# Attention stage of a transformer block on one core: the four output chunks of a quad of units spread over four iterations

## The chip, the cores and the metric

The kernel runs on one core of a Trainium2 chip. The metric is the time of one execution on the device, in microseconds (us), lower is better.

## The reference

`x` has shape (4, 512, 128). It is normalised per token; the result goes into an attention branch and into a mixture-of-experts branch, and both are added to `x`:

```python
xn = _layernorm(x, axis=-1)
x = x + attention(xn) + experts(xn)
# attention, 16 heads of 8, keys and values through a latent of 32
scores = einsum('bhqd,bhkd->bhqk', qh, kh) * scale
scores = clip(nan_to_num(scores), -1e4, 1e4) * exp(-1e-4 * |i - j|)
attn = softmax(scores, axis=-1)
out = einsum('bhqk,bhkd->bhqd', attn, vh)      # then @ Wo
# experts: top 2 of 8, exact gelu, hidden size 512, then layer norm
```

## The kernel before

All data stays in fp32; products of scores are made of bf16 parts. A first part (to about 129 us) normalises, projects, routes tokens to experts and runs the experts' matmuls. The second part, which the change touches, is the attention; it takes the branch `fast == 1` on every engine. POOL gathers the experts' results meanwhile, and VectorE, beside its share of attention, normalises the sum per batch.

**Units.** There are 4 x 16 = 64 pairs of batch and head. A *group* is 4 heads (16 groups). Each group is done in two halves, and each half has two tiles of 128 keys (`HALVES = ((0, 3), (1, 2))`). One head's half is a *unit*: 128 units, 8 a group. Four units of one half are a *quad*: 32 quads. Units 8g to 8g+3 and 8g+4 to 8g+7 are the two quads of group g. In the traces unit n is found by counting: the loads of L626 come two a unit, from unit 0 at 128.64 us.

**One loop, four engines.** Each engine runs a loop over n, written out at build time; n is called an iteration, or unit n.
- TensorE, `scores(n)` (L626): two matmuls 128x512 into banks 2(n mod 3) and the next, so three units have scores at a time. Before them it waits for `fast_probs`, that is, for the exponential of unit n-3.
- VectorE (L1043): two multiplications correct the decay in these banks in place.
- ScalarE (L811): one exponential 128x1024 writes `probs_fast`, two buffers of one quad each; it signals `fast_probs`. The first exponential of a quad waits for `fast_used`, given when the quad two before (same buffer) is done with.
- TensorE, `outputs(quad, chunk)` (L645): a quad's probabilities times values. There are four chunks: two key tiles by two halves of the queries, each with four matmuls of 9 x 256, one for each head, side by side in the output bank, and each in two passes. Chunk 0 waits for the quad's four exponentials, and in a group's first quad for `fast_heads` as well. Chunk 3 signals `fast_used`.
- ScalarE, `heads(group)` (L785): copies the output bank to `out_heads` ahead of the exponential of unit 8g+12, once both of the group's quads are used; it signals `fast_heads`.
- TensorE, `turn(group)` (L659), at iteration 8g+17: four transposes of the copied heads, after which VectorE divides by the sums (L1031, L1033).

Three batches' attention is turned and projected inside the loop, too: transposes L603 at iterations 101, 109 and 125, their copy by ScalarE (L789) ahead of the exponentials of units 100, 108 and 124, matmuls L610 two iterations after L603, and an addition by VectorE (L1014), for which the next turn waits (`out_ready`). VectorE takes statistics (L986, L992, L994) after units 58, 66, 92 and 98, and roots and scalings (L1000 to L1007) from units 84, 88, 106 and 109. After unit 127 the loop goes on for 20 iterations to finish the last chunks and turns.

Waits are on semaphores, and each engine works strictly through its own list, so what stands behind a waiting instruction waits with it. The order around the change is set by the loop at the end of TensorE's branch (L661 to L678): in each iteration come the scores of unit n, then the chunks that the tuple `((0,), (1, 2), (3,), ())` names, taken at `at`, the place of n in its quad counted from n = 6, then a turn where one is due, then the transposes and the projection of a batch.

Of the kernel before, what the change touches and what calls it, by code (L numbers as in the profile page):

```python
# [65 lines left out]
def build(nc, x_tiles, chain, w_up, w_router, rest, weights, decay, fold, mend, out):  # L66
    with ExitStack() as ctx:
# [169 lines left out]
        def batch_at(n, units, step=0):  # L237
            return units.index(n - step) if n - step in units else None
# [233 lines left out]
        def _(pe):  # L472
# [128 lines left out]
            def turn_attention(b):  # L601
                for t in range(QT):
                    last = nc.tensor.transpose(ps[:, TURN_BANK, t * P:(t + 1) * P],  # L603
                                               attn[:, b * QT + t, :, :].rearrange("p h d -> p (h d)"), ident)
                last.then_inc(attnT_psum, 1)

            def project_attention(b):
                pe.wait_ge(attnT_ready, b + 1)
                for t in range(QT):
                    last = nc.tensor.matmul(ps[:, TURN_BANK, t * D:(t + 1) * D], attnT[:, b * QT + t, :], wo_sb,  # L610
                                            start=True, stop=True)
                last.then_inc(wo_psum, 1)
# [3 lines left out]
            with pe.If(fast == 1):  # L616
                def scores(n):
                    group, half, g = n // (2 * GROUP), n // GROUP % 2, n % GROUP
                    b, h = divmod(group * GROUP + g, HEADS)
                    if n % (UNITS // B) == 0:  # L620
                        pe.wait_ge(rows_in[b % 2], (b // 2 + 1) * len(PRODUCTS) * 2 * 16)
                    if n >= SCORE_SLOTS:
                        pe.wait_ge(fast_probs, n - SCORE_SLOTS + 1)
                    for k in range(2):
                        keys = HALVES[half][k] * P
                        nc.tensor.matmul(ps[:, 2 * (n % SCORE_SLOTS) + k, :], k_rows[:, b % 2, h, keys:keys + P],  # L626
                                         q_rows[:, b % 2, h, :], start=True, stop=True).then_inc(fast_scores, 1)

                def outputs(quad, chunk):
                    k, side = divmod(chunk, 2)  # L630
                    queries = slice(side * S // 2, (side + 1) * S // 2)
                    group, half = divmod(quad, 2)
                    tile = HALVES[half][k]
                    first_tile, last_tile = (half, k) == (0, 0), (half, k) == (1, 1)
                    if chunk == 0:
                        pe.wait_ge(fast_probs, (quad + 1) * GROUP)
                    if first_tile and side == 0:
                        if group:
                            pe.wait_ge(fast_heads, group)
                        else:  # L640
                            pe.wait_ge(v_ones, 1)
                            pe.wait_ge(out_clear, 1)
                    for g in range(GROUP):
                        b, h = divmod(group * GROUP + g, HEADS)
                        last = nc.tensor.matmul(ps[32 * g:32 * g + VW, OUT_BANK, queries], v_sb[:, b * QT + tile, h, :],  # L645
                                                probs_fast[:, quad % 2, g, k * S + queries.start:k * S + queries.stop],
                                                start=first_tile and side == 0,
                                                stop=last_tile and side == 1, skip_group_check=True)
                    if chunk == 3:
                        last.then_inc(fast_used, 1)  # L650

                def turn(group):
                    pe.wait_ge(fast_heads, group + 1)
                    if group:
                        pe.wait_ge(fast_done, group)
                    if group - 1 in PROJECT_GROUPS:
                        pe.wait_ge(out_ready, PROJECT_GROUPS.index(group - 1) + 1)
                    for t in range(QT):
                        last = nc.tensor.transpose(ps[:, TURN_BANK, t * P:(t + 1) * P], out_heads[:, t * P:(t + 1) * P], ident)  # L659
                    last.then_inc(fast_outT, 1)  # L660

                for n in range(UNITS + 5 * GROUP):
                    if n < UNITS:
                        scores(n)
                    quad, at = divmod(n - GROUP - 2, GROUP)
                    if 0 <= quad < QUADS:
                        for chunk in ((0,), (1, 2), (3,), ())[at]:
                            outputs(quad, chunk)
                    group, at = divmod(n - TURN_AFTER, 2 * GROUP)
                    if 0 <= group < GROUPS and at == 0:  # L670
                        turn(group)
                    if (b := batch_at(n, PROJECT_AT)) is not None:
                        pe.wait_ge(fast_done, GROUPS if b == B - 1 else PROJECT_GROUPS[b] + 1)
                        turn_attention(b)
                    if (b := batch_at(n, MULTIPLY_AT)) is not None:
                        project_attention(b)
# [471 lines left out]
```

## Time and profile before

| what | value |
|---|---|
| median of 3 runs | 300.53 us (299.96 to 301.22) |
| the profiled execution's own time | 301.67 us |
| its span | 299.9 us |
| busy: TensorE matmul, weight loads | 250.9 us, 140.1 us |
| busy: VectorE, ScalarE, POOL | 227.9, 203.0, 167.9 us |
| mean granted clock of TensorE | 0.945 |
| exponentials (L811), 128 | 124.8 us, 1029 ns each |
| corrections (L1043), 256 | 112.9 us, 495 ns each |
| chunks (L645), 1024 records, scores (L626), 232 records | 74.5 us, 71.5 us |

PE is TensorE's matmul, PEld its weight load, DVE VectorE, ACT ScalarE. Times in a timeline count from the span's start; an entry such as [0.43 <-ACT shared L811] says how long the engine sat idle before the row, and what ended it. Neighbouring instructions of one kind are merged into one row with their count. Matmuls are pipelined, so the length of one holds its latency, and the step from one start to the next says what it occupies. Some matmul records are missing from the trace (232 of 256 for L626); the weight loads are complete.

### The profile page before, as it was taken

The page shows a single profiled execution, that of the slowest core. Times are in us where ns is not written, and L with a number is a line of the kernel's source. Part 1 is how long each engine was busy: PE and PEld are TensorE (multiplying, and loading weights), DVE is VectorE, ACT ScalarE, POOL GpSimd, SP SyncE. Part 2 cuts the span into 40 slices and gives each one's busy share as a digit, 9 for nine tenths or more (in the row PEclk, how much of TensorE's full clock was granted, in tenths as well). Part 3 has the DMA queues.
Part 4 walks back from the last instruction along what each step waited for, and adds up shares of the span by engine and source line. Part 5 has one row for each costly group of instructions (what it writes and reads, how often), then busy time and mean ns, then how long its engine had stood idle before and what let it go on. Part 6 is the DMA issues. An engine that isn't in the chain of part 4 may idle for free.

```text
span 299.9 us, 6073 instructions
## 1 busy us (share of the span) xinstructions
PE 250.9 (84%) x2161; PEld 140.1 (47%) x2185; DVE 227.9 (76%) x585; ACT 203.0 (68%) x348; POOL 167.9 (56%) x158
## 2 busy tenths in 40 slices
PE   0394457989999999969999999989999598969883
PEld 0282033979999999922222233322233023332342
DVE  3718987587777777677888888889889987998831
ACT  1556506446666665668999999988997588769840
POOL 9296707447464557968899999995305711050000
PEclk9998957899999999998999999999999789999996
DMA  6992501242222323125111531115000000000001
GB/s 212 469 388 70 164 21 44 72 159 74 79 70 70 71 71 68 35 88 185 47 35 28 169 96 31 35 52 175 11 2 2 1 0 2 35 7 31 2 35 42
DMA packets 14065, 24.37 MB, mean 81 GB/s; under 512 B 2240, under 2 KB 11104, under 8 KB 13648
## 3 DMA queue, kind: packets, MB, share of 16 engines
q1 hardware_dynamic: 11424, 19.03, 17.8%
q0 software_dynamic: 2272, 4.66, 6.4%
q8 instruction: 19, 0.31, 0.4%
q10 hardware_dynamic: 336, 0.25, 0.3%
q14 instruction: 14, 0.11, 0.1%
HBM read 12.99 MB, written 4.65 MB: 59 GB/s over the span
## 4 chain that ended last, share of the span: by engine, by line
PE 57%; DVE 23%; ACT 11%; issue 5%; DMA 2%; another core or an unknown queue 1%; ACTq 0%; DVEq 0%
PE ps L645 13%; PE ps L626 12%; PE ps L572 11%; PE ps L583 11%; ACT shared L811 9%; DVE ps L1043 8%; PE ps L659 2%; DMA wvl<-w_router 2%; DVE panels L1007 2%; PE ps L493 2%; DVE shared L908 2%; PE ps L561 1%; PE ps L610 1%; PE ps L485 1%; DVE panels L1014 1%
## 5 line engine op out<-in xcount | busy, mean ns | idle before, releaser
L811 ACT ACTIVATE shared<-ps 128x1024 f32<-128x1024 f32 x128 | 124.8, 1029 | 21.3 <-DVE ps L1043 18.6
L1043 DVE TENSOR_TENSOR ps<-ps,mend_sb 128x128 f32<-128x128 f32 (+3 forms) x256 | 112.9, 495 | 19.8 <-PE ps L626 15.3
L626 PE MATMUL ps<-stacked 128*128 128x512 bf16 x232 | 71.5, 392 | 15.1 <-ACT shared L811 12.3
L645 PE MATMUL ps<-shared,v_sb 128*9 128x256 f32 x1024 | 74.5, 388 | 0.0
L774 ACT ACTIVATE shared<-ps,shared 128x128 f32<-128x128 f32 x156 | 44.6, 369 | 32.4 <-PE ps L572 32.4
L307 POOL DMA_INDIRECT shared<-xn_scr,source_i x39 | 42.0, 1076 | 39.1 <-PE ps L561 28.3
L927 DVE COPY shared<-panels 128x1156 f32 x39 | 36.3, 930 | 14.6 <-issue 14.6
L626 PEld LDWEIGHTS ps<-stacked 128*128 128x128 bf16 x256 | 17.1, 98 | 58.8 <-ACT shared L811 36.2
L572 PE MATMUL ps<-shared 128*128 128x128 f32 x312 | 42.3, 279 | 1.3 <-DVE shared L964 1.2
L583 PE MATMUL ps<-shared 128*128 128x128 f32 x312 | 42.2, 279 | 0.3 <-ACT shared L774 0.3
L645 PEld LDWEIGHTS ps<-shared,v_sb 128*9 128x9 f32 x1024 | 18.8, 89 | 48.1 <-issue 36.3
L572 PEld LDWEIGHTS ps<-shared 128*128 128x128 f32 x312 | 38.8, 195 | 2.0 <-DVE shared L964 1.6
L583 PEld LDWEIGHTS ps<-shared 128*128 128x128 f32 x312 | 38.8, 196 | 0.5 <-ACT shared L774 0.5
L316 POOL DMA_INDIRECT panels<-y_scr,y_row x32 | 31.2, 974 | 7.9 <-issue 5.2
L346 POOL TENSOR_TENSOR panels<-panels,rest_sb 128x512 f32<-128x512 f32 x4 | 5.1, 1271 | 31.9 <-DVE panels L1007 31.9
L972 DVE TENSOR_TENSOR y_rows<-ps,shared 128x128 f32<-128x128 f32 x39 | 11.3, 291 | 8.0 <-PE ps L583 7.5
L785 ACT COPY out_heads<-ps 128x512 f32<-128x512 f32 x16 | 9.3, 584 | 6.4 <-PE ps L645 6.4
L659 PE MATMUL ps<-chain_sb,out_heads 128*128 128x128 f32 x64 | 9.7, 275 | 3.1 <-DVE panels L1014 2.3
L561 PE MATMUL ps<-chain_sb,shared 128*128 128x128 f32 x39 | 11.2, 286 | 1.1 <-DMA shared<-xn_scr,source_i 1.1
L749 ACT ACTIVATE qT_sb<-ps 128x512 f32<-128x512 f32 x4 | 2.5, 614 | 14.2 <-PE ps L512 14.2
L964 DVE COPY shared<-ps 128x128 f32<-128x128 f32 x39 | 11.0, 282 | 0.4 <-PE ps L561 0.3
L659 PEld LDWEIGHTS ps<-chain_sb,out_heads 128*128 128x128 f32 x64 | 7.7, 141 | 7.3 <-issue 3.7
(146 smaller groups left out, 245.7 us busy)
## 6 DMA issues: line engine op xcount, KB each, us to landing
stacked<-parts SPq DMA_DIRECT2D x48, 128.0 KB
panels<-weights SPq DMA_DIRECT2D x1, 4624.0 KB, 18.2
y_scr<-y_rows SPq DMA_DIRECT2D x19, 128.0 KB
x_sb<-x_tiles SPq DMA_DIRECT2D x4, 256.0 KB, 4.8
xn_scr<-x_sb SPq DMA_DIRECT2D x1, 1024.0 KB, 7.2
xnT<-x_tiles SPq DMA_DIRECT2D x1, 1024.0 KB
out<-panels SPq DMA_DIRECT2D x4, 256.0 KB, 2.3
shared<-xn_scr,source_i POOLq DMA_INDIRECT x39
```

The costliest lines, as they stand in the source:

```text
L307: nc.gpsimd.indirect_dma_start(x_rows[:, i % X_SLOTS, :], None, xn_scr, bass.IndirectOffsetOnAxis(ap=source_i[:, i:i + 1], axis=0)).then_i ...
L316: nc.gpsimd.indirect_dma_start(gathered[:, c, t, :], None, y_scr, bass.IndirectOffsetOnAxis(ap=y_row[:, at:at + 1], axis=0)).then_inc(y_ba ...
L561: nc.tensor.transpose(ps[:, 4 + i % 2, 0:P], x_rows[:, i % X_SLOTS, :], ident).then_inc(xT_psum, 1)
L572: last = nc.tensor.matmul(ps[:, s, c * P:(c + 1) * P], panel[:, i % 4, c * P:(c + 1) * P], x_cols[:, s, :], start=True, stop=True)
L583: last = nc.tensor.matmul(ps[:, Y_BANKS[i % 2], 0:D], hidden[:, i % 2, c, :], panel[:, i % 4, F + c * D:F + (c + 1) * D], start=(c == 0), ...
L626: nc.tensor.matmul(ps[:, 2 * (n % SCORE_SLOTS) + k, :], k_rows[:, b % 2, h, keys:keys + P], q_rows[:, b % 2, h, :], start=True, stop=True) ...
L645: last = nc.tensor.matmul(ps[32 * g:32 * g + VW, OUT_BANK, queries], v_sb[:, b * QT + tile, h, :], probs_fast[:, quad % 2, g, k * S + quer ...
L659: last = nc.tensor.transpose(ps[:, TURN_BANK, t * P:(t + 1) * P], out_heads[:, t * P:(t + 1) * P], ident)
L774: last = nc.scalar.activation(hidden[:, i % 2, c, :], ps[:, i % 2, c * P:(c + 1) * P], ACT.Gelu, bias=panel[:, i % 4, 2 * F + D + c:2 * F ...
L811: nc.scalar.activation(probs_fast[:, quad % 2, g, :].rearrange("p (k q) -> p k q", k=2), ps[:, 2 * (n % SCORE_SLOTS):2 * (n % SCORE_SLOTS) ...
L927: nc.vector.tensor_copy(panel[:, i % 4:i % 4 + 1, :], panels[:, bass.ds(e, 1), :]).then_inc(panel_ready, 1)
L1043: last = nc.vector.tensor_tensor(scores, scores, mend_sb[:, S - reach:], ALU.mult)
```

## The change

The four chunks of a quad run at four iterations, one each: chunk 2 moves from the second to the third, chunk 3 from the third to the fourth, which had none.

```diff
                     quad, at = divmod(n - GROUP - 2, GROUP)
                     if 0 <= quad < QUADS:
-                        for chunk in ((0,), (1, 2), (3,), ())[at]:
-                            outputs(quad, chunk)
+                        outputs(quad, at)
                     group, at = divmod(n - TURN_AFTER, 2 * GROUP)
```

TensorE's list at iterations 12 to 14, before; L626 are scores, L645 chunks (x4 is one chunk, x8 two):

```order
L626 MATMUL ps<-stacked 128x512 [waits fast_probs]
L626 MATMUL ps<-stacked 128x512
L645 MATMUL ps<-shared,v_sb 9x256 x4
L626 MATMUL ps<-stacked 128x512 [waits fast_probs]
L626 MATMUL ps<-stacked 128x512
L626 MATMUL ps<-stacked 128x512 [waits fast_probs]
L626 MATMUL ps<-stacked 128x512
L645 MATMUL ps<-shared,v_sb 9x256 [waits fast_heads,fast_probs]
L645 MATMUL ps<-shared,v_sb 9x256 x3
```

And with the change:

```order
L626 MATMUL ps<-stacked 128x512 [waits fast_probs]
L626 MATMUL ps<-stacked 128x512
L645 MATMUL ps<-shared,v_sb 9x256 x4
L626 MATMUL ps<-stacked 128x512 [waits fast_probs]
L626 MATMUL ps<-stacked 128x512
L645 MATMUL ps<-shared,v_sb 9x256 x4
L626 MATMUL ps<-stacked 128x512 [waits fast_probs]
L626 MATMUL ps<-stacked 128x512
L645 MATMUL ps<-shared,v_sb 9x256 [waits fast_heads,fast_probs]
L645 MATMUL ps<-shared,v_sb 9x256 x3
```

In iteration 12 chunk 2 stands where chunk 3 stood, and chunk 3 now comes after the scores of unit 13, ahead of those of unit 14.

TensorE's list at iterations 16 to 18, where a turn (L659) stands, before:

```order
L626 MATMUL ps<-stacked 128x512 [waits fast_probs]
L626 MATMUL ps<-stacked 128x512
L645 MATMUL ps<-shared,v_sb 9x256 x4
L626 MATMUL ps<-stacked 128x512 [waits fast_probs]
L626 MATMUL ps<-stacked 128x512
L659 MATMUL ps<-chain_sb,out_heads 128x128 [waits fast_heads]
L659 MATMUL ps<-chain_sb,out_heads 128x128 x3
L626 MATMUL ps<-stacked 128x512 [waits fast_probs]
L626 MATMUL ps<-stacked 128x512
```

And with the change:

```order
L626 MATMUL ps<-stacked 128x512 [waits fast_probs]
L626 MATMUL ps<-stacked 128x512
L645 MATMUL ps<-shared,v_sb 9x256 x4
L626 MATMUL ps<-stacked 128x512 [waits fast_probs]
L626 MATMUL ps<-stacked 128x512
L645 MATMUL ps<-shared,v_sb 9x256 x4
L659 MATMUL ps<-chain_sb,out_heads 128x128 [waits fast_heads]
L659 MATMUL ps<-chain_sb,out_heads 128x128 x3
L626 MATMUL ps<-stacked 128x512 [waits fast_probs]
L626 MATMUL ps<-stacked 128x512
```

The turn, which followed the scores of unit 17 directly, now follows chunk 3, and there are as many chunks and turns as before. The lists of ScalarE, VectorE, POOL and SP hold the same instructions in the same order in both kernels.

## Rows read from the trace of the kernel before

**Rows 1.** The page: busy time of each engine, and the chain by engine.

```profile
PE 250.9 (84%) x2161; PEld 140.1 (47%) x2185; DVE 227.9 (76%) x585; ACT 203.0 (68%) x348; POOL 167.9 (56%) x158
...
PE 57%; DVE 23%; ACT 11%; issue 5%; DMA 2%; another core or an unknown queue 1%; ACTq 0%; DVEq 0%
```

**Rows 2.** Stretches that begin and end at a group's first scores, L626 alone.

```profile
core 0: us, PE busy (x) PEld busy (x), PEclk, DMA share, GB/s
146.93:191.31 44.38, 21.71 (x73) 5.37 (x80) 1.00 0.23 66
191.31:210.12 18.81, 8.71 (x29) 1.98 (x32) 1.00 0.32 100
210.12:227.86 17.74, 8.64 (x29) 2.15 (x32) 1.00 0.01 3
227.86:243.27 15.41, 5.51 (x14) 0.96 (x16) 0.78 0.01 2
243.27:253.97 10.70, 4.60 (x15) 1.07 (x16) 1.00 0.01 2
```

**Rows 3.** Timeline of TensorE's weight loads, units 36 to 43 (start, length, merged).

```profile
169.23 0.11 PEld L626 LDWEIGHTS ps<-stacked 128*128 128x128 bf16 x2 [0.43 <-ACT shared L811]
169.77 0.12 PEld L645 LDWEIGHTS ps<-shared,v_sb 128*9 128x9 f32 x8 [0.42 <-issue]
170.32 0.55 PEld L626 LDWEIGHTS ps<-stacked 128*128 128x128 bf16 x4 [0.43 <-ACT shared L811]
...
172.03 0.11 PEld L626 LDWEIGHTS ps<-stacked 128*128 128x128 bf16 x2 [0.61 <-ACT shared L811]
172.56 0.55 PEld L645 LDWEIGHTS ps<-shared,v_sb 128*9 128x9 f32 x16 [0.42 <-issue]
173.54 0.11 PEld L626 LDWEIGHTS ps<-stacked 128*128 128x128 bf16 x2 [0.43 <-issue]
174.08 0.12 PEld L645 LDWEIGHTS ps<-shared,v_sb 128*9 128x9 f32 x8 [0.42 <-issue]
174.63 0.11 PEld L626 LDWEIGHTS ps<-stacked 128*128 128x128 bf16 x2 [0.43 <-issue]
174.86 0.57 PEld L659 LDWEIGHTS ps<-chain_sb,out_heads 128*128 128x128 f32 x4
...
176.59 0.11 PEld L626 LDWEIGHTS ps<-stacked 128*128 128x128 bf16 x2 [0.43 <-issue]
```

**Rows 4.** Timeline of ScalarE, units 36 to 43.

```profile
170.46 0.59 ACT L785 COPY out_heads<-ps 128x512 f32<-128x512 f32 x1 [0.34 <-PE ps L645]
170.94 3.78 ACT L811 ACTIVATE shared<-ps 128x1024 f32<-128x1024 f32 x4
174.93 4.07 ACT L811 ACTIVATE shared<-ps 128x1024 f32<-128x1024 f32 x4 [0.20 <-DVE ps L1043]
```

**Rows 5.** Timelines of TensorE and of VectorE, units 88 to 96.

```profile
235.25 0.60 PE L626 MATMUL ps<-stacked 128*128 128x512 bf16 x2 [2.38 <-ACT shared L811]
...
229.79 1.22 DVE L1000 TENSOR_TENSOR newton<-rstd 128x4 f32<-128x4 f32 x1
...
243.70 0.91 DVE L1043 TENSOR_TENSOR ps<-ps,mend_sb 128x128 f32<-128x128 f32 x2 [0.76 <-PE ps L626]
```

**Rows 6.** Timelines of weight loads and of ScalarE, units 100 to 103.

```profile
247.83 0.11 PEld L626 LDWEIGHTS ps<-stacked 128*128 128x128 bf16 x2 [0.43 <-ACT shared L811]
...
251.57 0.11 PEld L626 LDWEIGHTS ps<-stacked 128*128 128x128 bf16 x2 [1.12 <-ACT shared L811]
...
250.00 0.59 ACT L789 COPY kT_sb<-ps 128x512 f32<-128x512 f32 x1 [0.19 <-PE ps L603]
250.49 3.78 ACT L811 ACTIVATE shared<-ps 128x1024 f32<-128x1024 f32 x4
```

**Rows 7.** Timeline of weight loads at unit 127 and after.

```profile
286.23 0.97 PEld L610 LDWEIGHTS ps<-rest_sb,kT_sb 128*128 128x128 f32 x8 [0.43 <-issue]
...
288.24 0.42 PEld L659 LDWEIGHTS ps<-chain_sb,out_heads 128*128 128x128 f32 x4 [0.80 <-issue]
```

## The prediction

> **What bounds the kernel now.** I read the page first: TensorE is busy for 84% of the span, VectorE 76, ScalarE 68, and the chain that ended last lies 57% on TensorE with 11% on ScalarE [rows 1]. No engine is full, so the bound has to be read inside the stage that the change touches. The stretches by group of 8 units come next [rows 2]: five groups take 44.38 us, 8.88 each, two more take 17.74, 8.87 each; the two groups with statistics on VectorE take 9.41 each, and the later ones 15.41 and 10.70. A group of 8.87 us is the regular case, and I take it apart.
>
> TensorE's weight loads tell where each piece of its program begins [rows 3]. The load at 169.23 belongs to the scores of unit 36, the first unit of a second quad. From the scores and one chunk to the next scores is 1.09 us (173.54 to 174.63), from the scores and two chunks 1.51 (172.03 to 173.54). Units 37 and 38, one without a chunk and one with, take 1.71 (170.32 to 172.03), of which 0.18 is a wait: that load sat idle 0.61 us until ScalarE had finished, where loads behind a chunk otherwise sit idle 0.43. So scores alone cost 1.71 - 0.18 - 1.09 = 0.44. A turn costs 176.59 - 174.63 - 0.44 - 1.09 = 0.43. TensorE's own demand in a group is then 2 x (1.09 + 1.51 + 1.09 + 0.44) + 0.43 = 8.69, and with the wait of 0.18 it is 8.87, the measured period. **The regular group is bound by TensorE's order, with one short wait for ScalarE in it.**
>
> Where does that wait come from? Unit 36's scores are loaded at 169.23, its chunk 3 (of the quad before) at 169.77 [rows 3]. Chunk 3's signal lets ScalarE copy the heads at 170.46, the exponential of unit 36 follows at 170.94 [rows 4] and lasts 1.03; 0.05 after its end, at 172.03, TensorE may load the scores of unit 39, which take the same score banks. The path is 0.54 + 0.69 + 0.48 + 1.03 + 0.05 = 2.79 long, TensorE's work beside it 1.09 + 0.44 + 1.09 = 2.62: 0.17 of wait, as seen.
>
> **The change, part by part.** It removes and adds no arithmetic: 128 chunks as before. It moves chunk 2 behind the next unit's scores, and chunk 3 likewise. VectorE, ScalarE, POOL and SP keep their order and their instructions, and no DMA is moved.
>
> (a) Switches. Two chunks together cost 1.51 - 1.09 = 0.42 for the second, and one set apart costs 1.09 - 0.44 = 0.65. So splitting the pair costs 0.23 a quad. TensorE's demand in a group becomes 8 x 1.09 + 0.43 = 9.15, 0.46 more. I have no row for a turn that directly follows a chunk; between nothing extra and one more switch (0.1, half of the 0.23) I take nothing, since loads from one matmul shape to another behind a chunk sit idle 0.43 whichever follows [rows 7]: the turn pays the switch that the scores would have paid.
>
> The Trainium skill (TensorE: Matmul & The Clock Gate, "The mechanism" in Part 3) says that TensorE pulls a weight load ahead of matmuls in flight when it goes to rows that don't conflict or to the background buffer. By that rule the added switches would be free and the group's demand would stay near 8.69; the trace speaks against it here, since every first load of a chunk stands idle 0.42 us behind scores [rows 3].
>
> (b) The release. Chunk 3 now stands behind the scores of unit 37, not of unit 36, so the path above grows by one unit: 1.09 + 2.79 = 3.88. Queued behind the waiting heads copy on ScalarE is the exponential of unit 36, and for that wait, three units on, the scores of unit 39. TensorE's work beside the path is 3 x 1.09 = 3.27. The wait becomes 0.61. The first quad of a group has no copy: its exponential waits for chunk 3 directly, 1.09 + 0.54 + 0.69 + 1.03 + 0.05 = 3.40, against 3.27 + 0.43 (the turn falls there) of work. No wait there, with 0.3 to spare.
>
> A regular group: 9.15 + 0.61 = 9.76, **0.89 more than 8.87**. VectorE's work of about 7.5 us a group fits inside, and ScalarE catches up, its exponentials following each other by 0.92 (four take 3.78 [rows 4]).
>
> (c) The irregular groups. In the first 16 units the wait arises once and one switch is added: +0.6. With statistics, ScalarE now waits for chunk 3 longer than for VectorE, so 9.76 takes the place of 9.41: +0.35 each, +0.7 for two. From unit 84 VectorE is the bound (square roots at 1.22 us for a tiny operation, while POOL works [rows 5]); the change has by then added 0.2 in that group, and the 0.7 that it would add is swallowed: TensorE stood idle 2.38 us there [rows 5]. Out of that stretch TensorE comes at a lower clock (mean 0.78 of full [rows 2], so partly at 1.2 GHz after that idling) and is late for VectorE by 0.76 [rows 5]; chunk 3 and its switch cost +0.3 (0 to 0.8). At unit 100 ScalarE has a second copy, of the turned attention, that TensorE's chunk 3 now precedes: scores at 247.83, exponential at 250.49, 2.66 later [rows 6]; one chunk more ahead of those transposes is +0.65, less what TensorE saves around it: +0.5. Units 104 to 115 wait for VectorE and for the projection's bank: +0.2. Units 112 to 115 end with one chunk fewer done, -0.4. One more regular group +0.9, unit 124 as unit 100, +0.7. In the tail the chunk left over runs while TensorE would sit idle (0.80 us before the turn at 288.24 [rows 7]): -0.4.
>
> Sum: 0.6 + 5 x 0.89 + 0.7 + (0.9 + 0.2) + 0.3 + 0.5 + 0.2 - 0.4 + 0.9 + 0.7 - 0.4 = 8.65, the (0.9 + 0.2) being the groups from 210.12 to 227.86. I take 8.5. The profiled execution took 301.67 us (span 299.9), which gives 310.2 for it. It is 1.14 above the median of the runs, 300.53; against the median the forecast is **309.0 us**. A difference under 0.5% (1.5 us) can't be told from none here.
>
> **The rivals.**
> - *Only the switches cost.* If ScalarE's late release is hidden, a regular group takes 9.15, +0.28, and groups bound elsewhere nothing: 5 x 0.28 + 2 x 0.28 + about 0.6 for the rest = 2.6, so 303.1. For it: ScalarE is busy for only 68% [rows 1]. Against: the 2.79 path is met to 0.01 by the present wait. 0.07.
> - *Only the release costs.* With added switches free, the group takes 9.76 - 0.46 = 9.30, +0.43, half of the forecast: 304.8. The rule quoted above on weight loads would make this the outcome. Against: the 0.42 idle loads. 0.07.
> - *The clock falls more.* TensorE will wait 0.6 us in each group and longer from unit 84. The stretch that idles now shows 0.78 [rows 2]; at half speed a unit's 1.09 becomes 2.18. Three more such units cost 3.3: 312.3. Against: a wait of 0.6 is far below the 2.38 us seen before the fall. 0.06.
> - *Faster.* Place: the first scores of each quad. They come 0.42 earlier, since the pair no longer stands before them, and ScalarE's stall there (four exponentials begun at 170.94, the next four at 174.93, so 3.99 where 4 x 0.92 = 3.68 would do [rows 4]) goes: 0.3 a quad, 0.6 a group, 8 regular groups, 4.8 us: 295.7. It decides only if TensorE's demand falls below 8.87 with the split, that is if a split pair costs under 0.09 instead of 0.23, and if the buffer is free earlier than chunk 3 says. 0.02. The two effects cancelling within 0.5%: 0.03.
>
> **How the numbers follow.** The forecast's own case has 0.75; its terms could each be off by a few tenths: with the turn's extra switch (10 x 0.1) and the upper end after the slow clock (0.5) it reaches 310.5 to 311; with 0.75 instead of 0.89 a group and nothing at 100 and 124 it is about 306.5. The range takes in the case of free switches and leaves out the others, 0.18: **304.7 to 311.3**. Slower by over 0.5% 0.95, within 0.5% 0.03, faster 0.02.
>
> **What would show it.** In the changed profile a regular group takes 9.7 to 9.8 us; the weight loads of scores and chunks alternate at 1.09; the scores of unit 39 sit idle about 1.04 (0.43 + 0.61) for ScalarE; the heads copy begins 2.3 after the scores of unit 36 instead of 1.2. ScalarE's wait for L645 before the copy grows from 0.34 [rows 4] to about 1 us, and one of about 0.7 appears before the first exponential of the quad without a copy. A copy that is late without a late load of unit 39 would be the first rival; loads of chunks not idle behind scores the second; a granted clock under 1.00 between 146 and 200 us the third. A period at or under 8.87 would refute the sum.

## The result, and the profile after

The changed kernel takes 306.88 us (306.8 to 307.08, 4 runs) where the kernel before, run beside it, takes 300.88 (299.96 to 301.37): a ratio of 1.0204, with a 95% interval of 1.0177 to 1.0232. It is 6.0 us slower; 309.0 was forecast, 304.7 to 311.3 the range.

| | before | after |
|---|---|---|
| profiled execution, its span | 301.67, 299.9 us | 306.8, 305.0 us |
| mean granted clock of TensorE | 0.945 | 0.972 |
| regular group of 8 units | 8.87 us | 9.79 us |
| ScalarE idle ahead of the heads copies (L785, now L784) | 6.4 us | 14.9 us |

The changed kernel's page: busy time by engine, and the chain that ended last by engine. One line of code has gone, so ScalarE's and VectorE's lines are one lower (L810 for L811, L784 for L785); the scores' L626, the chunks' L645 and the turn's L659 are the same.

```profile
PE 257.6 (84%) x2185; PEld 134.2 (44%) x2185; DVE 228.8 (75%) x585; ACT 200.6 (66%) x348; POOL 166.8 (55%) x158
...
PE 66%; DVE 18%; ACT 8%; issue 4%; DMA 3%; POOL 0%; ACTq 0%; DVEq 0%
```

The chain has moved further onto TensorE (66% for 57%) and off ScalarE and VectorE [rows 1]. By group, in stretches cut as in [rows 2], scores alone:

```profile
core 0: us, PE busy (x) PEld busy (x), PEclk, DMA share, GB/s
145.82:194.79 48.97, 24.15 (x80) 4.94 (x80) 1.00 0.21 62
194.79:214.37 19.58, 9.66 (x32) 1.98 (x32) 1.00 0.29 89
214.37:233.96 19.59, 9.66 (x32) 1.98 (x32) 1.00 0.01 3
233.96:248.08 14.12, 5.45 (x16) 1.02 (x16) 0.88 0.01 2
248.08:259.32 11.24, 4.82 (x16) 1.07 (x16) 1.00 0.01 1
```

Five regular groups take 48.97 us, 9.79 each. The groups with statistics (194.79 to 214.37) take the same 9.79, and the next two as well; only then does VectorE set the time again. The timeline of TensorE's weight loads at units 36 to 44, which answers to [rows 3]:

```profile
170.24 0.11 PEld L626 LDWEIGHTS ps<-stacked 128*128 128x128 bf16 x2 [0.43 <-issue]
170.78 0.12 PEld L645 LDWEIGHTS ps<-shared,v_sb 128*9 128x9 f32 x8 [0.42 <-issue]
171.33 0.11 PEld L626 LDWEIGHTS ps<-stacked 128*128 128x128 bf16 x2 [0.43 <-issue]
...
172.41 0.11 PEld L626 LDWEIGHTS ps<-stacked 128*128 128x128 bf16 x2 [0.43 <-issue]
173.25 0.15 PEld L645 LDWEIGHTS ps<-shared,v_sb 128*9 128x9 f32 x8 [0.73 <-issue]
174.12 0.11 PEld L626 LDWEIGHTS ps<-stacked 128*128 128x128 bf16 x2 [0.71 <-ACT shared L810]
...
176.83 0.12 PEld L645 LDWEIGHTS ps<-shared,v_sb 128*9 128x9 f32 x8 [0.42 <-issue]
177.38 0.42 PEld L659 LDWEIGHTS ps<-chain_sb,out_heads 128*128 128x128 f32 x4 [0.43 <-issue]
...
180.03 0.11 PEld L626 LDWEIGHTS ps<-stacked 128*128 128x128 bf16 x2 [0.43 <-issue]
```

Scores and single chunks alternate at 1.09. The load at 172.41 is unit 38's, and behind it chunk 0 waits for the heads copy (idle 0.73 where 0.42 is the switch), then the load of unit 39's scores for ScalarE (0.71): 3.88 lies between 170.24 and 174.12, where it was 2.80. From 170.24 to the same place of the next group, 180.03, is 9.79. The turn at 177.38 stands behind a chunk and is idle 0.43, as the scores would be. ScalarE in the same stretch, as in [rows 4]:

```profile
172.55 0.58 ACT L784 COPY out_heads<-ps 128x512 f32<-128x512 f32 x1 [1.00 <-PE ps L645]
173.04 3.78 ACT L810 ACTIVATE shared<-ps 128x1024 f32<-128x1024 f32 x4
177.58 3.77 ACT L810 ACTIVATE shared<-ps 128x1024 f32<-128x1024 f32 x4 [0.76 <-PE ps L645]
```

The heads copy begins 2.31 after unit 36's scores and is idle 1.00 before it, for 0.34; the first exponential of the other quad is idle 0.76 for chunk 3, where it had waited 0.20 for VectorE.

### The profile page after: what moved, and what is told of

It is laid out like the page before. It is cut to its first block, busy times and chain, and to the rows that moved or that the text cites. A ratio compares the mean times of both kernels' runs of the same rounds, so it can differ in the third digit from the quotient of the medians.

```text
span 305.0 us, 6097 instructions
## 1 busy us (share of the span) xinstructions
PE 257.6 (84%) x2185; PEld 134.2 (44%) x2185; DVE 228.8 (75%) x585; ACT 200.6 (66%) x348; POOL 166.8 (55%) x158
## 4 chain that ended last, share of the span: by engine, by line
PE 66%; DVE 18%; ACT 8%; issue 4%; DMA 3%; POOL 0%; ACTq 0%; DVEq 0%
PE ps L645 18%; PE ps L626 17%; PE ps L572 11%; PE ps L583 11%; ACT shared L810 6%; DVE ps L1042 4%; PE ps L659 3%; DMA wvl<-w_router 2%; PE ps L493 2%; PE ps L561 2%; DVE shared L907 1%; DVE panels L1006 1%; PE ps L610 1%; PE ps L485 1%; ACT out_heads L784 1%
## 5 line engine op out<-in xcount | busy, mean ns | idle before, releaser
L810 ACT ACTIVATE shared<-ps 128x1024 f32<-128x1024 f32 x128 | 122.3, 1033 | 23.1 <-PE ps L645 11.5
L1042 DVE TENSOR_TENSOR ps<-ps,mend_sb 128x128 f32<-128x128 f32 (+3 forms) x256 | 114.1, 494 | 26.9 <-PE ps L626 26.2
L626 PE MATMUL ps<-stacked 128*128 128x512 bf16 x256 | 77.5, 386 | 11.3 <-ACT shared L810 10.9
L645 PE MATMUL ps<-shared,v_sb 128*9 128x256 f32 x1024 | 79.4, 385 | 2.9 <-ACT out_heads L784 2.9
L307 POOL DMA_INDIRECT shared<-xn_scr,source_i x39 | 41.1, 1053 | 38.4 <-PE ps L561 27.4
L626 PEld LDWEIGHTS ps<-stacked 128*128 128x128 bf16 x256 | 16.3, 97 | 59.9 <-ACT shared L810 40.4
L645 PEld LDWEIGHTS ps<-shared,v_sb 128*9 128x9 f32 x1024 | 15.9, 88 | 56.8 <-issue 55.9
L784 ACT COPY out_heads<-ps 128x512 f32<-128x512 f32 x16 | 9.4, 585 | 14.9 <-PE ps L645 14.9
L341 POOL TENSOR_TENSOR rstd<-newton,top 128x4 f32<-128x4 f32 x4 | 4.1, 1023 | 16.8 <-DVE newton L993 16.8
L659 PE MATMUL ps<-chain_sb,out_heads 128*128 128x128 f32 x64 | 10.5, 286 | 1.8 <-DVE panels L1013 1.1
```

Of the source, the lines that this page charges most:

```text
L307: nc.gpsimd.indirect_dma_start(x_rows[:, i % X_SLOTS, :], None, xn_scr, bass.IndirectOffsetOnAxis(ap=source_i[:, i:i + 1], axis=0)).then_i ...
L810: nc.scalar.activation(probs_fast[:, quad % 2, g, :].rearrange("p (k q) -> p k q", k=2), ps[:, 2 * (n % SCORE_SLOTS):2 * (n % SCORE_SLOTS) ...
L1042: last = nc.vector.tensor_tensor(scores, scores, mend_sb[:, S - reach:], ALU.mult)
```

## The experiments

Each experiment is an edit of the kernel before (of the changed one where it says so), and each is read first by one regular group, units 72 to 79. The first fence of an experiment is that stretch (its start and end, its length, then the scores' records in it and the granted clock), as in [rows 2]; a second one is its timeline of weight loads, as in [rows 3]; rows of other engines say so by their names. The kernel before ran beside them and had a median of 301.50, 301.57 and 300.71 us in the three series.

**A switch more, the release where it was.** Chunk 1 runs between the two score matmuls of its unit.

```diff
                     for k in range(2):
                         keys = HALVES[half][k] * P
+                        if k and n >= 7 and n % GROUP == 3:
+                            outputs(n // GROUP - 1, 1)
...
-                        for chunk in ((0,), (1, 2), (3,), ())[at]:
+                        for chunk in ((0,), (2,) if n < UNITS else (1, 2), (3,), ())[at]:
```

> The pair of chunks 1 and 2 is split inside its own iteration: chunk 1 goes between the two score matmuls of that unit, chunk 2 behind them, so there is one more switch pair a quad but chunk 3, and with it the release of the buffer and of the heads copy, stays where it was in the kernel before. Theory (switches 0.46 a group and release 0.44 a group, added up): a regular group takes 8.87 + 0.46 = 9.33 us, the wait before the scores of unit 39 stays at 0.17, time about 303.5 to 304.5. Rival 'only the late release costs': the group stays at 8.87 and the time at 300.9. Rival 'only the switches cost': the group takes as long as in the changed kernel, 9.79, and the time is near 306.9.

```profile
213.30:222.62 9.32, 5.00 (x16) 1.22 (x16) 1.00 0.03 9
```

```profile
168.04 0.10 PEld L628 LDWEIGHTS ps<-stacked 128*128 128x128 bf16 x1 [0.43 <-issue]
168.36 0.12 PEld L647 LDWEIGHTS ps<-shared,v_sb 128*9 128x9 f32 x8 [0.23 <-issue]
168.91 0.10 PEld L628 LDWEIGHTS ps<-stacked 128*128 128x128 bf16 x1 [0.43 <-issue]
169.23 0.12 PEld L647 LDWEIGHTS ps<-shared,v_sb 128*9 128x9 f32 x8 [0.23 <-issue]
169.78 0.11 PEld L628 LDWEIGHTS ps<-stacked 128*128 128x128 bf16 x2 [0.43 <-issue]
```

(L628 is the scores, L647 a chunk here.) The group takes 9.32, 0.45 more than before, as the theory has it; from 168.04 to 169.78 are 1.74 for a unit whose pair is split, where the pair took 1.51: 0.23 a switch pair, with nothing else moved. The time was expected at 303.5 to 304.5 and came out at 307.71 (ratio 1.0232, 1.0189 to 1.0275). The regular groups are right and the rest is not: the two groups with statistics take 20.35 us for 18.81, the first 16 units 18.68 with the clock at 1.00. Two places show in the trace. Unit 7 is the first whose scores are split; the second half reaches VectorE late, its correction begins at 135.62 and ends at 137.88, where in the second profile of the kernel before it is 135.62 and 136.52, and its exponential starts 1.28 later than there. In the first group with statistics a small VectorE instruction (newton<-mv, L994 before, L996 here) takes 1.15 for 0.17, which is no part of the split; the next experiment shows what holds it up.

**The release later, no switch more.**

```diff
-                        for chunk in ((0,), (1, 2), (3,), ())[at]:
+                        for chunk in ((0,), (1, 2), (), (3,))[at]:
```

> Chunk 3 alone runs one iteration later, the pair stays together: no switch is added. Theory: path of 3.88 us against 0.44 + 1.09 + 1.09 = 2.62 of TensorE's work beside it, so a wait of 1.26; a regular group takes 8.69 + 1.26 = 9.95, 1.08 more than before and more than in the changed kernel (9.79); time about 308 to 309. Rival 'only the switches cost': 8.87 a group and 300.9. Rival 'the release costs what it costs in the changed kernel, 0.44': 9.31 a group, about 304.

```profile
215.36:224.71 9.35, 4.49 (x16) 1.15 (x16) 1.00 0.01 2
```

```profile
169.98 0.55 PEld L626 LDWEIGHTS ps<-stacked 128*128 128x128 bf16 x4 [0.43 <-issue]
...
172.34 0.15 PEld L645 LDWEIGHTS ps<-shared,v_sb 128*9 128x9 f32 x8 [0.73 <-issue]
173.21 0.11 PEld L626 LDWEIGHTS ps<-stacked 128*128 128x128 bf16 x2 [0.72 <-issue]
```

9.35 a group, 0.48 more than before. My 9.95 was wrong by an error of counting: the unit whose chunk 3 left has scores alone, 0.44 and not 1.09, so the path is 0.44 + 2.79 = 3.23. The trace has 3.23, from 169.98 to 173.21. Against 2.62 of work that is a wait of 0.61, the same as in the changed kernel, and the rival that said so was right in its figure. The time is 307.66 (1.0184, 1.0128 to 1.024). The two groups with statistics take 21.95 us of it for 18.81, more than the release's 0.48 each. 1.48 of that is one instruction:

```profile
199.27 1.65 DVE L994 TENSOR_SCALAR newton<-mv 128x4 f32<-128x4 f32 x1
```

```profile
199.71 1.17 POOL L287 TENSOR_TENSOR folded<-folded,parts 128x512 f32<-128x512 f32 x1
```

VectorE's L994 took 0.17 in the first profile of the kernel before. Here it takes 1.65 and ends at 200.92, 0.04 after POOL's L287 does. It is the same in the split above (1.15) and in the second profile of the kernel before (0.67): both ended 0.04 after a POOL TENSOR_TENSOR. The second of the two groups has a granted clock of 0.90 besides.

These two decide the main question. One switch pair a quad costs 0.45 a group, the later release 0.48, and both together, in the changed kernel, 0.92. The times alone would not have decided it: 307.71, 307.66 and the changed kernel's 306.88 to 308.98 lie within 2 us of each other, since the stretches outside the regular groups differ as well.

**The pair is chunks 2 and 3.**

```diff
-                        for chunk in ((0,), (1, 2), (3,), ())[at]:
+                        for chunk in ((0,), (1,), (2, 3), ())[at]:
```

> Chunks 1; 2 and 3; none: the pair is chunks 2 and 3, as many switches as before, chunk 3 in its old iteration but behind chunk 2. Theory: the release is 0.42 later (path 3.21), but TensorE's work beside the path grows by the same chunk (1.51 + 0.44 + 1.09 = 3.04), so the wait stays 0.17, a regular group 8.87, the time within 0.5% of 300.9. Rival 'what costs is that a chunk stands behind the next unit's scores (chunk 2 does here too)': part of the change's 6 us, 302 to 304.

```profile
211.00:219.87 8.87, 4.66 (x16) 1.08 (x16) 1.00 0.03 11
```

8.87, the period of before, and a time of 299.99 (0.9953, 0.9918 to 0.9988). Three of its groups between units 32 and 55 take 9.1 to 9.6 in the profile, which I can't place. Moving chunk 2 behind the next scores costs nothing in itself, and a release that is 0.42 later costs nothing when TensorE has 0.42 more to do beside it.

**Two pairs.**

```diff
-                        for chunk in ((0,), (1, 2), (3,), ())[at]:
+                        for chunk in ((0, 1), (), (2, 3), ())[at]:
```

> Chunks 0 and 1 together in the first iteration, 2 and 3 together in the third: one switch pair a quad fewer than before, two fewer than in the changed kernel. Theory: demand 8.69 - 0.46 = 8.23 a group; the release path is 3.21 against 1.51 + 0.44 + 1.51 = 3.46, no wait; a unit's own round (scores, correction, exponential, 2.46) against 0.44 + 1.51 + 0.44 = 2.39 adds up to 0.14: a regular group takes 8.3 to 8.4, the time 296 to 297.5. Rival 'switches are free': 8.87 or more a group, since chunks in pairs only make the scores come less evenly, 300.9 to 303.

```profile
210.25:218.93 8.68, 4.55 (x16) 1.07 (x16) 1.00 0.07 23
```

```profile
218.94 0.11 PEld L626 LDWEIGHTS ps<-stacked 128*128 128x128 bf16 x2 [0.66 <-ACT shared L811]
```

```profile
215.54 1.02 ACT L811 ACTIVATE shared<-ps 128x1024 f32<-128x1024 f32 x1 [0.45 <-DVE ps L1043]
216.46 0.58 ACT L785 COPY out_heads<-ps 128x512 f32<-128x512 f32 x1
```

8.68, less than the 8.87 of before, so switches are not free; but not 8.3 to 8.4. The load at 218.94 is the scores of unit 80, idle 0.66 for ScalarE. The third fence is ScalarE: the exponential of unit 75 and, right behind it, the heads copy. The other regular groups of this profile are less even, from 8.68 to 9.24. Two executions took 296.1 and 297.48 us (the profiled one) at a mean clock of 0.956, two took 300.95 and 302.61 at 0.950 and 0.941; no ratio can be given.

**The same with VectorE's division earlier.** It was my first reading of that wait.

```diff
-                        for chunk in ((0,), (1, 2), (3,), ())[at]:
+                        for chunk in ((0, 1), (), (2, 3), ())[at]:
...
-                    if 0 <= group < GROUPS and at == 2:
+                    if 0 <= group < GROUPS and at == 1:
                         normalise(group)
```

> The two pairs of the run before, and VectorE's division by the sums (L1031, L1033) one unit earlier, into the 0.60 that VectorE sits idle before unit 75's correction. Theory (the 0.45 of wait that the two pairs left came from this division standing ahead of unit 76's correction): 8.3 to 8.5 a regular group instead of 8.68, time 1.5 to 3 us below the two pairs. Rival (the wait comes from a unit's round of 2.46 alone): 8.68 as before.

```profile
209.38:218.06 8.68, 4.33 (x15) 1.07 (x16) 1.00 0.05 16
```

8.68 again (8.68 to 8.75 in all its regular groups): that reading fell. The time is 297.57 (0.9872, 0.9828 to 0.9916), within the scatter of the run before. Unit 76's correction did come earlier, 1.02 after its scores' load for 1.51, and its exponential still waited 0.62 beyond the correction's end.

What holds it is ScalarE's own list, and not the release. In the two pairs the last matmul of chunk 3 ended at 216.18, the copy began at 216.46, 0.92 after the exponential of unit 75 had begun and with no idle time between (here 215.31 and 215.59). The path runs from unit 75's scores (load at 214.16) over their correction, the exponential of unit 75, the heads copy and the exponentials of units 76 and 77 to the scores of unit 80 at 218.94: 4.78. TensorE's work in that time is 0.44 + 1.51 + 0.44 + 1.51 + 0.44 = 4.34, which leaves 0.44 of wait, and the group has 0.45. The rival's figure of 8.68 came, but not from a unit's round alone.

**Four single chunks, one unit earlier** (an edit of the changed kernel).

```diff
-                    quad, at = divmod(n - GROUP - 2, GROUP)
+                    quad, at = divmod(n - GROUP - 1, GROUP)
                     if 0 <= quad < QUADS:
                         outputs(quad, at)
```

> The changed kernel with all four single chunks one iteration earlier (the quad's place is counted from n = 5): as many switches as the changed kernel, but chunk 3 stands where the kernel before has it. Theory: TensorE's demand 9.15 a group; the path from unit 36's scores to unit 39's is 2.79 against 3.27, no wait; the one wait left is chunk 0 for the end of the heads copy (0.54 + 0.69 + 0.59 + 0.11 = 1.93 after unit 36's scores, against 1.09 + 0.54 = 1.63): 0.30, so 9.45 a regular group, 0.34 under the changed kernel; time about 304. Rival 'only the switches cost': 9.79 a group and about 307. Rival 'only the release costs': 8.87 a group and about 301.

```profile
215.58:225.09 9.51, 4.39 (x14) 0.99 (x16) 1.00 0.02 7
```

```profile
173.59 0.15 PEld L645 LDWEIGHTS ps<-shared,v_sb 128*9 128x9 f32 x8 [0.73 <-ACT shared L810]
174.17 0.11 PEld L626 LDWEIGHTS ps<-stacked 128*128 128x128 bf16 x2 [0.43 <-issue]
...
202.72 0.15 PEld L645 LDWEIGHTS ps<-shared,v_sb 128*9 128x9 f32 x8 [1.32 <-ACT shared L810]
```

9.51 a group for the 9.45 expected, 0.28 under the changed kernel, with chunk 0 waiting for the copy as foreseen (0.73 at 173.59, 0.31 over the switch) and the scores of unit 38 right behind. The regular groups bear the theory out. The time does not: 309.85 (1.028, 1.0247 to 1.0313), 6 more than expected and above the changed kernel. The groups with statistics take 20.21 us and units 96 to 103 12.16, where the changed kernel takes 19.58 and 11.24. The row at 202.72 shows where it goes in the first of them: it is chunk 0 in unit 61's iteration, idle 1.32. It waits for the heads copy (202.03 to 202.61), and the copy does not wait for chunk 3, whose matmuls ended at 201.36, but begins 0.92 after the exponential of unit 59, which VectorE's statistics had delayed to 201.11. In the changed kernel chunk 0 stands behind the scores of unit 62, which go ahead meanwhile; here they stand behind it, at 203.30. The same wait of 1.32 stands before chunk 0 at unit 101, where the transposes of a batch and their copy queue behind it as well.

**Two pairs, early.** Chunk 3 is signalled a unit sooner than before.

```diff
-                        for chunk in ((0,), (1, 2), (3,), ())[at]:
+                        for chunk in ((0, 1), (2, 3), (), ())[at]:
```

> Chunks 0 and 1 in the first iteration, 2 and 3 in the second, none in the others: as few switches as the two pairs, and chunk 3 a whole unit ahead of where the kernel before has it. Theory (the 0.45 of wait that both runs with two pairs kept is the release: chunk 3, heads copy, two exponentials, then the scores of the first unit of the next quad): demand 8.23, release hidden behind the exponential of unit 35, a unit's own round of 2.46 against 1.51 + 0.44 + 0.44 leaves under 0.1: 8.3 to 8.45 a regular group, time 295 to 297. Rival (with bursts of scores VectorE and ScalarE set the pace): 8.7 or more a group, 297.5 to 301.

```profile
205.85:214.19 8.34, 4.16 (x15) 1.14 (x16) 1.00 0.04 15
```

```profile
164.44 0.11 PEld L626 LDWEIGHTS ps<-stacked 128*128 128x128 bf16 x2 [0.43 <-ACT shared L811]
...
165.96 0.55 PEld L626 LDWEIGHTS ps<-stacked 128*128 128x128 bf16 x4 [0.43 <-ACT shared L811]
166.90 0.11 PEld L626 LDWEIGHTS ps<-stacked 128*128 128x128 bf16 x2 [0.39 <-ACT shared L811]
```

8.34 a group, as expected, and 295.76 us (0.9852, 0.9818 to 0.9886): **this order beats both kernels**, by 1.5% the one before. Two units of scores follow each other at 165.96 with the loads pulled ahead, and the next load, at 166.90, has no wait beyond what a round takes (164.44 to 166.90 is 2.46). Its demand of 8.23 leaves 0.11 of waits.

The number came as the theory said, but the trace doesn't bear out the reason that it gave. The copy at unit 76 again begins 0.92 after the exponential of unit 75 (210.97 and 210.05), chunk 3 being over at 210.26, so an earlier release moved nothing. What this order changes is TensorE's work beside the path of 4.78 from unit 75's scores to unit 80's: it is 1.51 + 0.44 + 0.44 + 1.51 + 1.51 = 5.41 instead of 4.34, and the path is hidden.

**One and three.**

```diff
-                        for chunk in ((0,), (1, 2), (3,), ())[at]:
+                        for chunk in ((0,), (1, 2, 3), (), ())[at]:
```

> Chunk 0 in the first iteration, 1, 2 and 3 in the second: the same number of switches and nearly the same release (0.42 later from the start of its iteration, which begins 0.42 earlier). Theory: like the two early pairs, 8.3 to 8.45 a regular group. Rival (the longest piece between two scores decides, 1.93 here against 1.51): more than the two early pairs by 0.2 or more a group.

```profile
210.19:218.99 8.80, 4.08 (x15) 1.22 (x16) 1.00 0.01 2
```

```profile
171.65 0.11 PEld L626 LDWEIGHTS ps<-stacked 128*128 128x128 bf16 x2 [0.92 <-ACT shared L811]
```

8.80 (8.79 in its other regular groups), and 301.97 us (1.0035, 1.0015 to 1.0054): the rival's figure. As few switches and nearly the same release are not enough. Behind the short units the scores of unit 39 sit idle 0.92 (171.65), since three units of 0.44, 0.44 and 1.09 are over before a round of 2.46 is: 0.49 in this quad, and 0.06 in the one with the turn, which with the demand of 8.23 gives 8.78. So it is the run of short units, and not the longest piece as the rival had it, that shows in the trace.

**Both kernels once more.** 8.5 was forecast and the medians gave 6.0; the clocks of the two profiles differed. Nothing is edited in these two runs.

> The changed kernel once more, for the part that the sum had too high (+8.5 forecast, +6.0 measured). Theory (regular groups as forecast, the rest is where TensorE's clock happens to be at half in the profiled executions: 6.8 us at units 93 to 96, the last projection and units 5 to 7 before, less of it in the changed kernel's profile): 9.79 a regular group again, with low clock spells elsewhere than in the first profile, and times that differ by 1 us or more between executions. Rival (the change itself removes the spells): the same spells as in its first profile, none at units 5 to 7 and at the last projection, 3.4 us near unit 93.

> The kernel before once more, as the other half of that comparison. Theory: 8.87 a regular group, spells of low clock that move from one execution to another. Rival: the same spells as in its first profile, at units 5 to 7, 93 to 96 and the last projection.

The first 16 units and the last projection of the kernel before, in its first profile (the second fence is TensorE's matmuls):

```profile
128.63:146.93 18.30, 9.21 (x29) 2.18 (x32) 0.91 0.42 123
```

```profile
294.11 2.08 PE L610 MATMUL ps<-rest_sb,kT_sb 128*128 128x128 f32 x8 [0.67 <-ACT kT_sb L789]
```

The same of the changed kernel in its first profile:

```profile
127.71:145.82 18.11, 9.33 (x32) 1.98 (x32) 1.00 0.41 125
```

```profile
300.40 1.16 PE L610 MATMUL ps<-rest_sb,kT_sb 128*128 128x128 f32 x8 [0.68 <-ACT kT_sb L788]
```

The first 16 units, a regular group and units 88 to 95 of the kernel before, run again:

```profile
127.71:145.14 17.43, 8.31 (x29) 2.15 (x32) 1.00 0.43 129
208.79:217.66 8.87, 4.21 (x14) 1.07 (x16) 1.00 0.02 5
226.54:241.29 14.75, 5.05 (x14) 0.94 (x16) 0.88 0.01 2
```

And of the changed kernel, run again:

```profile
128.71:147.48 18.77, 9.71 (x29) 2.03 (x32) 0.91 0.39 121
216.04:225.83 9.79, 4.60 (x15) 0.99 (x16) 1.00 0.02 6
235.62:250.15 14.53, 5.68 (x14) 1.06 (x16) 0.77 0.01 2
```

The regular groups repeat to 0.01. The low clock does not stay where it was: for the first 16 units the kernel before has 0.91 and then 1.00, the changed kernel 1.00 and then 0.91, and each pays 0.7 to 0.9 where it is 0.91 (18.30 for 17.43, 18.77 for 18.11). Units 88 to 95 cost 15.41 at 0.78 and 14.75 at 0.88, 14.12 at 0.88 and 14.53 at 0.77. The last projection's L610 took 2.08 at half clock in the first profile before and 1.16 after. The spells move and the rival falls. In the second series the changed kernel takes 308.98 (1.0236, 1.0195 to 1.0277), 7.4 more than the 301.57 beside it.

## Why the prediction was right, and what was off

**The bound.** Right. The regular group is TensorE's order plus one wait for ScalarE; the experiments move it by the two terms named, and the two add.

**(a) The switches.** 0.46 forecast, 0.45 measured alone. The turn behind a chunk costs no further switch: it is idle 0.43 as forecast. The prediction quoted a rule of the Trainium skill (TensorE: Matmul & The Clock Gate, "The mechanism" in Part 3), that a weight load to rows that don't conflict or to the background buffer is pulled ahead of matmuls in flight, and took free switches to be what it would mean here. Between these two shapes no load is pulled ahead (idle 0.42 to 0.43 at each switch); within one shape the trace agrees, as the four score loads at 165.96 in the early pairs show, which lie within 0.55 though a unit's scores take 0.44.

**(b) The release.** The path of 3.88 and the wait before unit 39 are met to the hundredth. Idle time sits in two places and not in one: chunk 0 takes 0.31 of it, waiting for the copy, and unit 39's load 0.28, so the mark of 1.04 for that one load was wrong while the sum of waits was right. The prediction left out that chunk 0 in a group's first quad waits for the copy; in the changed kernel that wait lies within the path of 3.88 and costs nothing more, in the single chunks one unit earlier it is the one that counts. A regular group: 9.76 forecast, 9.79 measured.

**(c) The irregular groups.** Compared at equal clocks, by stretch (forecast in brackets; the terms of each stretch are added, and 116 to 119 is 0.67 of a regular group's 0.89, 120 to 123 the remaining 0.22):

- units 0 to 15: +0.7, or +0.5 at the low clock (+0.6)
- units 16 to 55: 48.97 - 44.38 = +4.6 (+4.45)
- units 56 to 71: +0.8 against the first profile of before, +0.3 against the second, where L994 took 0.67 for 0.17 (+0.7)
- units 72 to 95: +1.2, 19.59 + 14.12 less 8.87 + 8.88 + 14.75 (+1.4); the 0.7 that VectorE was to swallow was swallowed only after unit 88
- units 96 to 103: 11.24 - 10.70 = +0.5 (+0.5)
- units 104 to 119: 22.78 - 22.44 = +0.3 (+0.5)
- units 120 to 126: 9.26 - 8.30 = +1.0 (+0.9)
- the tail, from unit 127's scores to the end: 13.61 against 14.08 in the second profile of before, -0.5 (-0.4)

With the 0.7 and the 0.8 these come to 8.6, the sum said 8.65. Each stretch is taken from the profile whose clock fits, so 8.6 is no whole execution's difference.

**The step that was off** is the last one: carrying the sum over to the medians as if the clock were the same. In the profiles the gap is 5.1. The missing 3.5 is 0.93 that the kernel before lost ahead of unit 0 (128.64 for 127.71), 0.8 to 0.9 in the first 16 units, 0.65 at units 72 to 95, and 1.1 in the tail, all in stretches where its clock was lower than in the changed kernel's profile. The first series had four executions of the changed kernel, all at 0.972, and the profiled one of before had 0.945; for the others of before beside it, which gave the 6.0, no clock is on record. The second series gives 7.4. Executions at the highest clock of either compare likewise: 306.9 at 0.972 against 299.6 and 299.77 at 0.971, 7.2 us. So the clock can account for about half of the 2.5 between 8.5 and 6.0. Of the 1.3 that remain, up to 0.5 can be the stretch of L994; for the rest no run shows a place.

**The rivals.** "Only the switches" and "only the release" each hold half. The clock rival did not come: the longer waits brought no low clock in the regular groups (1.00 in all of them), and the mean in the first series was higher than before. The later release alone did bring one, in the second group with statistics (0.90). The faster rival asked for a cheaper split than 0.09; the split costs 0.23.

## What to carry over

Where an engine alternates between two shapes of matmul, count the alternations before spreading the work evenly: here each pair of switches costs 0.23 us beside 0.42 for the chunk itself. For a signal that other engines queue behind, compare its path with the work that the signalling engine has in the meantime; it costs only the excess, so it can be a chunk late for nothing (the pair 2 and 3) or a unit late for 0.5. Look in the trace, too, for what released the engine that waits: the two pairs seemed to wait for chunk 3 and in fact waited for ScalarE's own list. Gathering can go too far as well: two pieces of two beat one and three, because three units in a row can't be shorter than a round through the engines.

## What the runs showed of the hardware

TensorE's clock falls at changing places in one and the same program. Over the 42 executions beside the three series the kernel before took 299.4 to 302.72 us, with a mean clock of 0.960 to 0.971 in the eleven up to 300.34 and of 0.945 to 0.960 in the others. A profile's irregular stretches should be read with the granted clock beside them; between the two profiles of this kernel the spans differ by 1.5 us, and the stretch of units 112 to 119, at 1.00 in one and 0.86 in the other, alone by 1.5.

Small VectorE instructions can wait for POOL. In the first group with statistics L994 (128x4) took 0.17 us in both profiles of the changed kernel, where POOL ran nothing beside it. In six other profiles a POOL TENSOR_TENSOR ran beside it; there it took 0.25 to 1.65 and ended 0.04 after POOL's instruction. The 1.22 of L1000 in [rows 5] is like it: it ends 0.02 after POOL's L348, and the same line took 0.15 at 224.79, where POOL ran nothing.
